# W_in centred ahead of the projection, tile sums scaled when added, and most columns of x taken from a transposed copy

## The reference

```python
h = rmsnorm(layernorm(x), g_res) @ W_in + b_in
c = rmsnorm(ctx, g_init)[:, :512]              # a running decayed sum over the rows of c: scan
x = x + h + scan(c)[plug]                      # plug: a row number, from sums over the mask
x = x + gelu(layernorm(x) @ w1 + b1) @ w2 + b2 # 512 -> 2048 -> 512
```

## Time and profile before

| | |
|---|---|
| median of three runs | 858.76 us (854.37 to 859.01) |
| the profiled execution: its time | 854.02 us |
| its span, first to last instruction | 851.9 us |
| mean granted clock of TensorE | 0.998 of full speed |
| busy: TensorE / VectorE / ScalarE / GpSimd | 827.5 / 315.2 / 293.1 / 267.8 us |
| moved by DMA | 73.17 MB |

### The profile page before, as it was taken

One profiled execution on the slowest core, in us unless ns is written; L12 is line 12 of the kernel. 1 busy time (PEld: TensorE's weight loads), 2 busy tenths in 40 slices (PEclk: granted clock), 3 DMA queues, 4 the chain that ended last, 5 costly groups with the idle time before them and its releaser, 6 DMA issues.

```text
span 851.9 us, 10840 instructions
## 1 busy us (share of the span) xinstructions
PE 827.5 (97%) x3758; PEld 679.9 (80%) x3758; DVE 315.2 (37%) x523; ACT 293.1 (34%) x506; POOL 267.8 (31%) x290
## 2 busy tenths in 40 slices
PE   4998999999999999999999999999999999999998
PEld 3776788788888888888888887888888888888886
DVE  5888862444342242414151424234113311241112
ACT  4674535542532235222622243223222322222221
POOL 6263666970162005310522044202500250011000
PEclk9999999999999999999999999999999999999999
DMA  9876798160214212241125021402300140010001
GB/s 235 278 212 189 249 240 307 50 165 7 75 50 122 49 49 74 72 99 38 43 82 132 0 74 49 97 0 95 53 1 1 50 89 9 0 49 1 1 1 49
DMA packets 35688, 73.17 MB, mean 86 GB/s; under 512 B 5796, under 2 KB 5796, under 8 KB 33768
## 3 DMA queue, kind: packets, MB, share of 16 engines
q1 hardware_dynamic: 26972, 61.54, 22.1%
q0 software_dynamic: 4608, 8.39, 6.2%
q10 hardware_dynamic: 4080, 2.89, 1.2%
HBM read 48.92 MB, written 23.89 MB: 85 GB/s over the span
## 4 chain that ended last, share of the span: by engine, by line
PE 86%; DVE 4%; POOL 4%; issue 2%; ACT 2%; DMA 1%; SPq 0%; POOLq 0%; DVEq 0%; ACTq 0%
PE acc L781 14%; PE acc L782 14%; PE acc L783 14%; PE h_bank L781 13%; PE h_bank L783 13%; PE h_bank L782 13%; PE t_bank L824 2%; DVE cl L944 1%; PE t_bank L776 1%; DMA x_next<-x_part 1%; POOL w_lo L478 1%; POOL cl L497 1%; POOL w_lo L484 1%; POOL x_next L505 1%; DMA xa_even<-in_x_dram 1%
## 5 line engine op out<-in xcount | busy, mean ns | idle before, releaser
L1144 DVE TENSOR_TENSOR h_lo<-g_f,h_hi 128x512 fp32r<-128x512 f32 x128 | 100.9, 788 | 452.0 <-ACT g_f L728 452.0
L726 ACT ACTIVATE h_hi<-h_bank,b_c 128x512 fp32r<-128x512 f32 x128 | 88.1, 688 | 434.4 <-PE h_bank L783 429.6
L781 PE MATMUL h_bank<-xt_hi,w_hi 128*128 128x512 f32 x512 | 201.9, 394 | 0.0
L781 PE MATMUL acc<-w_hi,h_hi 128*128 128x512 f32 x512 | 199.8, 390 | 0.0
L783 PE MATMUL h_bank<-xt_hi,w_lo 128*128 128x512 f32 x512 | 199.4, 389 | 0.0
L782 PE MATMUL h_bank<-xt_lo,w_hi 128*128 128x512 f32 x512 | 199.3, 389 | 0.0
L783 PE MATMUL acc<-w_hi,h_lo 128*128 128x512 f32 x512 | 199.2, 389 | 0.0
L782 PE MATMUL acc<-w_lo,h_hi 128*128 128x512 f32 x512 | 199.2, 389 | 0.0
L782 PEld LDWEIGHTS h_bank<-xt_lo,w_hi 128*128 128x128 f32 x512 | 96.2, 188 | 20.8 <-issue 1.2
L781 PEld LDWEIGHTS h_bank<-xt_hi,w_hi 128*128 128x128 f32 x512 | 96.1, 188 | 20.8 <-issue 1.2
L783 PEld LDWEIGHTS h_bank<-xt_hi,w_lo 128*128 128x128 f32 x512 | 96.1, 188 | 20.1
(11 more groups left out here) (145 smaller groups left out, 706.3 us busy)
## 6 DMA issues: line engine op xcount, KB each, us to landing
x_next<-x_part SPq DMA_DIRECT2D x8, 1024.0 KB, 4.8
out_dram<-x_cur SPq DMA_DIRECT2D x32, 256.0 KB, 2.1
w_raw<-in_L_ffn_w_dram SPq DMA_DIRECT2D x6, 1024.0 KB, 9.0
scan_table<-cl SPq DMA_DIRECT2D x6, 896.0 KB
ch<-in_ctx_dram SPq DMA_DIRECT2D x20, 256.0 KB, 2.9
cl<-in_ctx_dram SPq DMA_DIRECT2D x5, 1024.0 KB
xa_even<-in_x_dram SPq DMA_DIRECT2D x16, 256.0 KB, 5.2
xa_odd<-in_x_dram SPq DMA_DIRECT2D x16, 256.0 KB, 5.7
```

The source lines that it names most:

```text
L726: act.activation(h_hi[:, m % HB, :], h_bank[m % 2][:], ACT.Gelu, bias=b1_c[:, m:m + 1])
L781: nc.tensor.matmul(dst, a_hi, b_hi, start=first, stop=False)
L1144: dve.tensor_tensor(h_lo[:, m % HB, :], g_f32[:], h_hi[:, m % HB, :].bitcast(F32), ALU.subtract).then_inc(h_split, 1)
```

## The change

- The host also hands over `x_cols`: for each tile, x transposed in blocks of 128 columns, in the layout that the four transposes leave in PSUM. Tiles 3 to 31 (`from_host`) load it next to x, into 12 buffers in the still empty `w_raw` (`xc`). Tiles 0 to 2 are still transposed by TensorE, but from x itself.
- The mean is taken out of W_in instead of x: `sum_w_in` sums the rows of `g_res * W_in` with four products, `centre_w_in` subtracts a 512th of the sum from each row; then the high and low parts are made. The factor `ra` goes to `tile_add`, which becomes product times `ra` plus x. `tile_norm` and `na_bias` go.
- `tile_low` of the odd tiles from 3 on runs on GpSimd, the rest on VectorE. For host tiles both operands lie in SBUF.
- The sums of group 0 are written to `x_next` directly; their stores and the reload go. The clearing of `cl` and `ch_all` goes to VectorE. `scales` works on four tiles at once. Most mask and scan steps stand one tile earlier. GpSimd's steps at the end of the stage are spread over t = 14 to 28, between its low halves.

The diff, cut to its core:

```diff
+def from_host(t):
+    return t >= 3
+def low_on_pool(t):
+    return t % 2 == 1 and t >= 3
...
             def load_tile(t):
+                if from_host(t):
+                    m = HOSTED.index(t)
+                    if m >= XTR:
+                        wait_low(sp, HOSTED[m - XTR])
+                        sp.nop(nofuse=True)
+                    sp.dma_start(xc(t), x_cols[t, :, :]).then_inc(xc_loaded[m % XTR], 16)
                 sp.dma_start(xa(t), x_v[t // TI, :, t % TI, :]).then_inc(xa_loaded[t % XR], 16)
...
-                step(pool.tensor_tensor(ra[:, u], va_a[:, 0:n], neg_half[:, 0:n], ALU.pow))
-                step(pool.tensor_tensor(mr_a[:, 0:n], mv_a[:, u, 0], ra[:, u], ALU.mult))
-                pool.tensor_scalar(na_bias[:, u], mr_a[:, 0:n], -1.0, 1.0, ALU.mult, ALU.mult).then_inc(ra_ready, n)
+                pool.tensor_tensor(ra[:, u], va_a[:, 0:n], neg_half[:, 0:n], ALU.pow).then_inc(ra_ready, n)
+
+            def tile_low(t):
+                pool.wait_ge(x_hi, t + 1)
+                pool.tensor_tensor(h_lo[:, t % HB, :], xc(t), h_hi[:, t % HB, :].bitcast(F32), ALU.subtract).then_inc(xc_lo, 1)
...
             for t in range(NT):
+                if t + 2 < NT and low_on_pool(t + 2):
+                    tile_low(t + 2)
...
-                if t % 2 == 0 and t + 6 < NT:
-                    scales(t + 6, 2)
+                if t % 4 == 2 and t + 2 < NT:
+                    scales(t + 2, TI)
...
-            wait_apart(pool, table_stored, STORED + BLOCK_STORED * 2)
-            for i in range(TI):
-                add_context(0, i, 2)
-            for k in range(K):
-                low_w1(0, k, 1)
-            group_scale(0)
+                if 14 <= t <= 17:
+                    pool.wait_ge(acc_read, t - 13)
+                    add_bias(t - 14)
+                if t == 18:
+                    pool.wait_ge(plug_ready, 1)
+                    gather_indices(0)
+                if t in (23, 24):
+                    if t == 23:
+                        wait_apart(pool, table_stored, STORED + BLOCK_STORED * 2)
+                    add_context(0, 2 * (t - 23), 2)
+                    add_context(0, 2 * (t - 23) + 1, 2)
+                if t in (25, 26):
+                    low_w1(0, 2 * (t - 25), 1)
+                    low_w1(0, 2 * (t - 25) + 1, 1)
+                if t == 27:
+                    low_w2(0, 0, 2)
+                    low_w2(0, 1, 2)
+                if t == 28:
+                    group_scale(0)
...
             act.wait_ge(g_res_loaded, 16)
+            for k in range(K):
+                act.activation(g_wide[:, k, :], ones[:], ACT.Copy, scale=g_res_c[:, k:k + 1]).then_inc(g_made, 1)
+            for k in range(K):
                 act.wait_ge(win_loaded[k], 16)
-                act.activation(win_hi[:, k, :], win_raw[:, k, :], ACT.Copy, scale=g_res_c[:, k:k + 1]).then_inc(win_hi_done, 1)
+                act.activation(win_g[:, k, :], win_raw[:, k, :], ACT.Copy, scale=g_res_c[:, k:k + 1]).then_inc(win_scaled, 1)
             tile_high(0)
+            for k in range(K):
+                act.wait_ge(win_centred, k + 1)
+                act.activation(win_hi[:, k, :], win_raw[:, k, :], ACT.Copy).then_inc(win_hi_done, 1)
             for v, src in ((g_init_b, g_init[0:D]), (b_in_b, b_in), (b2_b, b2)):
                 act.dma_start(v[:], src.rearrange("(a n) -> a n", a=1).to_broadcast([P, D])).then_inc(small_loaded, 16)
...
             tile_high(1)
...
+            def sum_w_in():
+                for k in range(K):
+                    pe.wait_ge(g_made, k + 1)
+                    pe.wait_ge(win_loaded[k], 16)
+                    ins = nc.tensor.matmul(acc[3][:], g_wide[:, k, :], win_raw[:, k, :], start=(k == 0), stop=(k == K - 1))
+                ins.then_inc(win_summed, 1)
...
             transpose_first(0)
+            sum_w_in()
             transpose_first(1)
-            for t in range(3):
-                project(t)
-                transpose_first(t + 2)
-            for t in range(3, NT):
-                if t + 2 < NT:
+            for t in range(NT):
+                if t + 2 < NT and not from_host(t + 2):
                     transpose_first(t + 2)
-                if t == 3:
+                if t == 2:
                     mask_totals()
...
+            dve.memset(ch_all[:], 0.0).then_inc(zeroed, 1)
+            dve.memset(cl[:], 0.0).then_inc(zeroed, 1)
...
                 dve.wait_ge(h_used, t + 1)
-                dve.tensor_tensor(xa(t), p_bank[t % 3][:], xa(t), ALU.add).then_inc(acc_read, 1)
+                dve.wait_ge(ra_ready, t + 1)
+                u = t % XR
+                dve.scalar_tensor_tensor(x1(t), p_bank[t % 3][:], ra[:, u:u + 1], xa(t), ALU.mult, ALU.add).then_inc(acc_read, 1)
...
+            def centre_w_in(k):
+                if k == 0:
+                    dve.wait_ge(win_summed, 1)
+                dve.wait_ge(win_scaled, k + 1)
+                dve.scalar_tensor_tensor(win_raw[:, k, :], acc[3][:], -1.0 / D, win_g[:, k, :], ALU.mult, ALU.add)\
+                    .then_inc(win_centred, 1)
...
             tile_stats(0)
-            low_w_in((0, 1))
-            tile_stats(1)
-            low_w_in((2,))
             tile_low(0)
-            low_w_in((3,))
-            tile_stats(2)
-            tile_stats(3)
+            centre_w_in(0)
+            centre_w_in(1)
+            low_w_in(0)
+            centre_w_in(2)
+            low_w_in(1)
+            centre_w_in(3)
+            low_w_in(2)
+            low_w_in(3)
             tile_low(1)
-            tile_stats(4)
-            tile_stats(5)
+            for t in range(1, 6):
+                tile_stats(t)
             for t in range(NT):
                 if t > 0:
                     tile_add(t - 1)
-                if t + 2 < NT:
+                if t + 2 < NT and not low_on_pool(t + 2):
                     tile_low(t + 2)
...
+    laid['x_cols'] = _np.asarray(inputs['x']).reshape(NG, P, TI, K, P).transpose(0, 2, 4, 3, 1).reshape(NT, P, D)
```

More of the change, by code:

```diff
@@ L95, in left, with xattn_ffn @@
         self.n = self.entered + turns * self.per
-def xattn_ffn(nc, x, ctx, mask, w_in, b_in, g_res, g_init, w1, b1, w2, b2, out):
+def from_host(t):
+    return t >= 3
+def low_on_pool(t):
+    return t % 2 == 1 and t >= 3
+POOL_LOW = [t for t in range(NT) if low_on_pool(t)]
+DVE_LOW = [t for t in range(NT) if not low_on_pool(t)]
+TURNED = [t for t in range(NT) if not from_host(t)]
+HOSTED = [t for t in range(NT) if from_host(t)]
+XTR = 12
+def xattn_ffn(nc, x, x_cols, ctx, mask, w_in, b_in, g_res, g_init, w1, b1, w2, b2, out):
     x_v = x.rearrange("b (g p i) d -> (b g) p i d", p=P, i=TI)
@@ L177, in xa, with xc, wait_low, turned_bank @@
             return (xa_odd if t // 8 % 2 else xa_even)[:, t % 8, :]
+        def xc(t):
+            u = HOSTED.index(t) % XTR
+            q = 3 - u // K
+            return w_raw[:, u % K, q * D:(q + 1) * D]
+        def wait_low(engine, t):
+            if low_on_pool(t):
+                engine.wait_ge(xc_lo, POOL_LOW.index(t) + 1)
+            else:
+                engine.wait_ge(x_lo, DVE_LOW.index(t) + 1)
+        def turned_bank(t):
+            return first_bank[TURNED.index(t) % 3]
+        def x1(t):
+            return x_next[:, t, :] if t < TI else xa(t)
         b_in_b = sb("b_in_b", [P, D])
@@ L269, in xattn_ffn @@
         ra_ready = sem("ra_ready")
-        n_ready = sem("n_ready")
+        g_made = sem("g_made")
+        win_scaled = sem("win_scaled")
+        win_summed = sem("win_summed")
+        win_centred = sem("win_centred")
+        x_turned = sem("x_turned")
+        x_hi = sem("x_hi")
+        x_lo = sem("x_lo")
+        xc_lo = sem("xc_lo")
+        xc_loaded = [sem(f"xc_loaded{i}") for i in range(XTR)]
         n_b_ready = sem("n_b_ready")
@@ L308, in _ @@
         def _(sp):
+            for k in range(2, K):
+                sp.dma_start(win_raw[:, k, :], win_v[:, k, :]).then_inc(win_loaded[k], 16)
             sp.dma_start(xa(0), x_v[0, :, 0, :]).then_inc(xa_loaded[0], 16)
-            for k in range(K):
-                sp.dma_start(win_raw[:, k, :], win_v[:, k, :]).then_inc(win_loaded[k], 16)
             wait_apart(sp, mask_cleared, 1)
@@ L383, in _ @@
                     loaded += 1
[L384 to L389, removed]
                 if t == 19:
@@ L399, in _ @@
                 if t == 29:
+                    wait_low(sp, HOSTED[2 * XTR - 1])
+                    wait_low(sp, HOSTED[2 * XTR - 2])
                     load_w1(1)
@@ L402, in _ @@
             store_x1(NT - 1)
+            wait_low(sp, NT - 1)
+            wait_low(sp, NT - 2)
             load_w1(2)
@@ L516, in group_scale @@
                 pool.tensor_tensor(rb[:], va_b[:], neg_half[:], ALU.pow).then_inc(rb_ready, 1)
[L518 to L521, removed]
+            scales(0, 2)
+            scales(2, 2)
             for q in range(HP):
@@ L604, in _ @@
                           allow_slow_non_contiguous=True).then_inc(g_res_loaded, 16)
```

(13 more changed lines are left out.)

155 lines of the change are left out of this document (71 added, 84 removed).

## The result

The changed kernel takes 866.88 us (median of 4 runs, 865.63 to 867.23) against 856.99 for the kernel before on the same chip (854.37 to 859.01): a ratio of 1.0119, 95% interval 1.0095 to 1.0143. The forecast was 853, the range 843 to 861. The profiled execution took 865.63 us, with a span of 863.8.

What follows compares the result with a forecast made beforehand. VectorE was taken as the bound up to `tile_add(20)`, GpSimd's queue behind it. Feed-forward starts at 130.6 - 6.0 - 0.1 = 124.5 us; profiled 847.9, plus 4.7 for the median gives 852.6, given as 853, range 843 to 861.

Steps and rivals of the forecast that it cites:

- The mask steps move one tile ahead at their price.: VectorE from `tile_low(1)` to `tile_add(20)`: mask steps shift one tile earlier, with no change in cost.
- `tile_low` and the scans, 15 in all with 512 columns: VectorE up to `tile_add(20)`: nine low halves and six scans lose +0.13 us each beside GpSimd, +2.0 us.
- at the full price: Rival: VectorE and GpSimd block each other, 15 operations at +1.0 us for +0.13, +13 us, so 866; chance 0.12.
- The start: Up to `tile_low(1)`: column sums and centring of W_in make it start at 18.8 us, a loss of 4.1.
- the 12.0 taken near the lower end: Start: column sum of W_in ready at 12.0 us, taking 4.6 us from a range of 4.1 to 7.6.
- 0.6 in the range: VectorE up to `tile_add(20)`: second operation and factor `ra` in `tile_add` cost at most +0.6 us in all.
- From `tile_add(20)` on: Tail to the feed-forward stage: a chain through GpSimd's queue, gathers and norms takes 34.6 us, before 34.7.
- the two forecast waits of TensorE for GpSimd's `h_lo`: Tail: TensorE stalls for the low halves of tiles 27 and 29 behind the gathers, 2 to 3 us each.
- move as a block: Feed-forward stage: arithmetic unchanged, only counts in its waits change, so it keeps its 721.3 us.
- the transfers hidden: First stage: 36.4 MB at 358 GB/s take 102 us of 125, so no engine waits for a load.
- VectorE as the bound without long gaps: First stage: VectorE is full from `tile_low(1)` to `tile_add(20)`, with no long idle gap between.
- the removal of the waits for `h_hi`: VectorE up to `tile_add(20)`: 9.1 us of waits go, since host tiles need only a load and a free buffer.

Runs made afterwards that it cites:

- third experiment: Changed kernel with GpSimd's 15 low halves replaced by two memsets each, which write and read nothing: 861.46 us, ratio 1.0052 to the kernel before.
- fourth: Changed kernel with the sum of a tile as a plain addition, without the factor `ra`: 867.23 us, ratio 1.0114 to the kernel before.
- ninth: Changed kernel with the statistics of tiles 1 to 3 made while VectorE waits for the column sums of W_in: 862.80 us, ratio 1.0069.
- tenth experiments: Changed kernel with all low halves on VectorE and GpSimd's `g_init` products of block 0 and bias additions moved later: 861.60 us, ratio 1.0063.
- second experiment: Changed kernel with only the low halves of tiles 27, 29 and 31 back from GpSimd on VectorE: 865.65 us, ratio 1.0099.
- the one with 12 tiles on ScalarE: Changed kernel with all low halves on VectorE and the statistics of 12 tiles made on ScalarE: 856.36 us, ratio 1.0013.

## Why the prediction was wrong

**The step that failed is "The mask steps move one tile ahead at their price."** They cost 18.5 us instead of 9.8, 8.7 of the 17.7 us by which the forecast of the profiled time (847.9) missed. (The median missed by 14.3: it lay 1.3 us above the profiled run, where 4.7 were added.) The prediction had the right mechanism in hand, VectorE and GpSimd blocking each other, and counted the wrong operations: it took `tile_low` and the scans, 15 in all with 512 columns, at +0.13, because they are large. Those came out near it: together 13.5 us, forecast 13.3. The steps of 26 columns were not counted. They pay what is left of GpSimd's operation, about 1 us, whatever their own length, so 0.2 us becomes 1.2. The rival "at the full price" had the price and the sign right, and named the wrong operations for it: its 15 lost about 0.14 us each. That its time of 866 came out is luck, since the small steps, the start and the tail make up the sum in their place. The chance of 0.12 for slower was too small. The price stood in the earlier trace rows; that a small step pays it too stood in the trace of before at 39.37 us and was not looked at.

Of the rule in the Trainium skill, "SBUF — State Buffer", section "SBUF: two separate sides", the prediction used half. The page says that the port pair is held for a whole instruction against a VectorE operation with two SBUF inputs, and also against one in a 2-port performance mode. The one-input steps that stood for 1.2 us would fall under the second half. Its condition that GpSimd must be reading is stated for two SBUF inputs alone, and the third experiment agrees with both parts: under a memset the two-input step took 0.19 us, and the one-input steps stood to its end. No run shows the mode itself.

What the runs show of this cause: with GpSimd's whole-tile operations gone from the stage the small steps are back at 8.6 us and the time falls by 0.74%; with memsets for its low halves it falls by 0.67%. It falls on VectorE's scans, low halves from SBUF, one-hots and small steps. It does not fall on everything: in the changed kernel the 21 `tile_add`, with an operand in PSUM, took 15.8 us, 0.75 each, just as with GpSimd silent, and the 27 statistics 18.4 against 18.4. Which steps are hit changes with every shift of a few tenths (fourth, ninth and tenth experiments), so the price is best taken per GpSimd operation.

**The start** took 20.3 us, not 18.8. The column sums ran from 7.95 to 13.87 us (5.91 for eight records, within the 4.1 to 7.6 given), so the sum was ready 1.9 later than the 12.0 taken near the lower end:

```profile
7.95 5.91 PE L836 MATMUL acc<-win_raw,g_wide 128*128 128x512 f32 x8
```

The first two records take 1.92 us, like the two at 75.33 of the earlier trace rows, where the granted clock was 0.50; the shortest of the eight takes 0.59, their median 1.06. So most of the sum ran at the lower clock, and taking a value near the lower end was the mistake. The profile's clock column says 1.00 for these 6 us, which doesn't fit the records. x(0) was there at 7.08 instead of 6.5. The rest of that chain was 6.4 instead of 6.8. The experiment without the centring gives its price: 5.8 us. It and the collisions (0.74%, 6.3 us, priced in the kernel with all low halves on VectorE) are each more than half of the 9.9 us by which the kernel got slower.

**`tile_add`** costs 0.67 from start to start for 0.61: +1.1 us, of which the prediction left 0.6 in the range. Waits were 1.6 us for 0.8.

**From `tile_add(20)` on**, the chain of operations was the one forecast, but of the two forecast waits of TensorE for GpSimd's `h_lo`, 2 to 3 us each, one came, 5.2 us long. The tail came out at 37.8 for 34.6. From the table's store to the first gather took 7.5 us (103.15 to 110.69) where 5.5 was taken from a row of the feed-forward stage; in the same stage of the kernel before it was 7.5 as well (96.50 to 104.03), an upper bound, since GpSimd made factors there until 103.3; from GpSimd's factors (131.4) to the feed-forward stage it was 8.9 for 7.7. GpSimd's queue and the gather:

```profile
110.69 1.81 POOL L564 DMA_INDIRECT x_next<-scan_table,idx  x1 [5.97 <-DMA scan_table<-cl_next]
...
130.43 1.01 POOL L570 TENSOR_TENSOR rb<-va_b,neg_half 128x4 f32<-128x4 f32 x1
```

What the prediction did not see is that the stall for `tile_low(27)` is not the cause of that length: without it most of the wait moves to `n_rows` (second experiment).

**The feed-forward stage** did not move as a block: 723.5 us for 721.3. TensorE waits 2.41 us for the scan before the first carry, 1.80 before, and the clock is low for some 3 us behind it:

```profile
175.55 1.25 PE L859 MATMUL t_bank<-cl,band 128*128 128x512 f32 x2 [2.41 <-DVE cl L1006]
176.12 1.11 PE L840 MATMUL h_bank<-xt_hi,w_hi 128*128 128x512 f32 x1
177.02 0.63 PE L841 MATMUL h_bank<-xt_lo,w_hi 128*128 128x512 f32 x1
```

Products follow each other at 0.43 us there, at 0.23 in the kernel before at the same place. The scan was late because ScalarE waited 4.87 us for the load of `ch`. Why the clock falls there in all of these changed kernels but the one with 12 tiles on ScalarE, which waits 2.47 us and needs 722.0 for the stage, stays open.

**Right** were: the transfers hidden (no engine waited for a load of x or of its transposed copy between 20 and 141 us), VectorE as the bound without long gaps, GpSimd's low halves above 1.3 us (1.5 on average) and VectorE's from SBUF near 0.8 (0.82), and the removal of the waits for `h_hi`. VectorE's waits in the passage fell by 7.7 us (9.3 to 1.6). That gain was real, and three costs ate it: small steps +8.7, start +5.6, tail and feed-forward stage +5.3, which makes the 11.9 us of the span.

## What to carry over

Price a tile-wide GpSimd operation that reads SBUF at about 1 us of VectorE's time wherever VectorE's steps from SBUF to SBUF come up behind its start (the statistics excepted); one that only writes holds up the steps with one SBUF input alone. Look at where the two meet, and count VectorE's smallest steps first: they lose as much as the large ones and are the most exposed. Before moving work to GpSimd to relieve a full VectorE, compare 0.6 us saved an operation with that. A serial passage ahead of a full engine is paid for until the next bound shows (here 6 of 9.3 us, then the loads), so look for work of that engine to put into its gaps.

## Not expected of the hardware

- A VectorE step of 26 columns with one SBUF input takes 1.20 to 1.27 us beside a GpSimd operation on 512 columns (1.3 us) that reads SBUF, and 0.18 beside GpSimd's power on four columns (1.0 us). Beside GpSimd's memsets such a step stands until their end (0.30 and 0.39 us; one of 32 columns 0.53), while a step with two SBUF inputs runs under one in 0.19.
- VectorE's `bn_stats` on 512 columns, which also reads SBUF alone, was never held up: 27 of them took 18.4 us in the changed kernel, with GpSimd at work 45.6 of 82.3 us, and 18.4 with GpSimd silent. Nor was an addition with one operand in PSUM (21 took 15.8 us in both).
- TensorE's granted clock fell behind a wait of 2.41 us in one kernel and not behind one of 2.47 us in another.
